# Cross-attention in a decoder layer: the null key and value subtracted in the fold, two score banks, and one softmax pass over 16 heads

## The chip, the cores and the metric

One NeuronCore of a Trainium2 chip runs the whole layer. The metric is the device time of one execution in microseconds (us). TensorE is called PE below, VectorE DVE, ScalarE ACT, GpSimd POOL and the engine that issues the transfers SP.

## The reference, cut to what matters

The input x is 4 x 1024 rows of 256. Three blocks follow each other, each behind a layer norm and with a residual: a gated linear scan, a cross-attention with 16 heads of 64 over 64 context rows per batch, and a feed-forward block of 1024 hidden columns with quantised activations and ternary weights. The change is in the cross-attention:

```
q = heads(x @ Wq) * DH**-0.5;  k, v = heads(context @ Wkv)      # 64 keys and values per head
k = concatenate((null_kv[0], k));  v = concatenate((null_kv[1], v))   # one null key and value for all heads
attn = softmax(q @ k.T)                                         # over 65 keys
out = (attn @ v) @ Wout;  out = layernorm(out)
x = x + out;   x = x + ffn(layernorm(x))
```

## The kernel before, in words

The rows are 32 tiles of 128. Stage 1 (the scan, eight groups of four tiles) runs first. Then the **fold**: Wq is multiplied with the keys of each head, and the values with Wout, so that the scores of a tile are one product of the normed tile (256 wide) with a folded matrix M, and the attention's output one product of the probabilities with VW. M is kept as a high and a low part (Mhi, Mlo), and so is the tile (xT2hi, xT2lo): three products stand for one in float32. Per head M has J = 65 columns, 64 keys and the null key, which is the same for each batch. Its columns come from null_key (L996 on, on DVE). The null value goes through a selection matrix nvsel (L1017 on, 16 small DVE copies) and the product null_values (L1397) into VWnull.

Then stages 2 and 3 run as one software pipeline, stages2_3(n), n from -2 to 31, each engine in its own written order. Nothing is planned at run time: the order in each engine's function and the semaphores set everything. Step n does on PE, in this order: the scores of tile n+2 (two halves, each of two banks with 4 heads x 65 = 260 columns, 24 products in all, banks 0 to 3); the transposes of the probabilities of tile n (banks 4 and 5, L1510 and L1518) and of their null part (L1524); the gate and the up product of the feed-forward block for tile n-5 (gate_up, banks 0, 1 and then 2, 3); the attention's output of tile n (16 products with VW, L1534 and L1539, and one with VWnull, L1540); in even steps the transposes of two more tiles (L1412); and the down product of tile n-7. All scores, gate, up and down products have one line, L1270. Steps 0 to 4 ("filling") have no feed-forward work; there the second half of the scores stands behind the transposes.

DVE's step n is: for each half of tile n+2 the maximum over each head's 65 columns (L1068) and the subtraction of it (L1071), the low part of the null probabilities (L1174), in odd steps xT2lo (L1046), the sum of the exponentials of tile n+1 (L1080), statistics, the hidden layer of the feed-forward block (L1093) which reads the up product, its maximum (L1100), the statistics of the attention's output (L1198), small scales, and the residual (L1152). ACT takes the exponential (L843) of a tile once both halves are subtracted. POOL divides by the sum (L554, and L557 for the null part).

Which wait holds which bank matters here. PE's gate product waits until the first half's scores are subtracted, the up product until the second half's are:

```
pe.wait_ge(sim_sub, upto(2 * n + 5, 2 * T))      # before gate, banks 0 and 1
pe.wait_ge(sim_sub, upto(2 * n + 6, 2 * T))      # before up, banks 2 and 3
```

Of the kernel before, what the change touches and what calls it, by code (L numbers as in the profile page):

```python
# [19 lines left out]
F32 = mybir.dt.float32  # L20
F32R = mybir.dt.float32r
# [12 lines left out]
def decoder_layer(nc, x, ctx_in, w_qkva, gamma, Wq, Wkv, null_kv, Wout, ln_scale, ln_bias,  # L34
# [15 lines left out]
    BANKS_S = 4  # L50
    HB = H // BANKS_S
# [3 lines left out]
    assert (KD, GT, DH, MK, H, N // GN) == (2, 4, 64, 64, 16, 2) and BM == 256 and HB * J <= 512  # L55
# [4 lines left out]
    with ExitStack() as stack:  # L60
# [19 lines left out]
        NP = 5 * H  # L80
        VWnull = sbuf("VWnull", [NP, D], F32R)
        pTn = sbuf("pTn", [NP, P], F32R)
# [25 lines left out]
        nk_bc = sbuf("nk_bc", [P, DH])  # L108
        mnull = sbuf("mnull", [P, KD, H])
        nv = sbuf("nv", [P, 1])  # L110
# [20 lines left out]
        with ExitStack() as early:  # L131
            region_w = early.enter_context(nc.sbuf_tensor("region_w", [P, KD * B * H * J], F32))
# [10 lines left out]
        Mhi = sbuf("Mhi", [P, KD, B, H * J], F32R)  # L143
        Mlo = sbuf("Mlo", [P, KD, B, H * J], F32R)
        region_c = sbuf("region_c", [P, 3968])
# [4 lines left out]
        def carve(region, spec):  # L150
            views, at = {}, 0
            for name, n in spec:
# [12 lines left out]
                             ("nvsel", HC * NP), ("nq", FI // 2), ("nhT", FI // 2)])  # L165
        nvsel = c["nvsel"]
# [15 lines left out]
        def slot_of(h):  # L182
# [20 lines left out]
                             ("xn", 4 * D), ("e", 2 * H * J), ("p", 2 * (H * MK + NP)), ("pT", HC * P),  # L203
# [59 lines left out]
        nkwq_done = sem("nkwq_done")  # L263
        mnull_done = sem("mnull_done")
        mnull_put = sem("mnull_put")
        nvsel_zero = sem("nvsel_zero")
        fT_psum = sem("fT_psum")
# [6 lines left out]
        mnull_hi = sem("mnull_hi")  # L274
        xT2_lo_ready = sem("xT2_lo_ready")
        nv_set = sem("nv_set")
        vwn_psum = sem("vwn_psum")
        vwn_ready = sem("vwn_ready")
# [12 lines left out]
        max_done = sem("max_done")  # L291
        sim_sub = sem("sim_sub")
# [4 lines left out]
        pTn_psum = sem("pTn_psum")  # L297
        pT0_psum = sem("pT0_psum")
        pT1_psum = sem("pT1_psum")
        pTn_hi = sem("pTn_hi")  # L300
        pTn_ready = sem("pTn_ready")
        vwn_hi = sem("vwn_hi")
# [89 lines left out]
        def _(sp):  # L392
# [7 lines left out]
            def weight_T(i, wT):  # L400
# [22 lines left out]
            sp.dma_start(nk_bc[:, :], null_kv[0:1, :].broadcast_to([P, DH])) \  # L423
                .then_inc(null_loaded, 16)
            sp.dma_start(nv[0:DH, :], null_kv[1].rearrange("(d o) -> d o", o=1)) \
                .then_inc(null_loaded, 16)
# [65 lines left out]
        def _(pool):  # L492
# [19 lines left out]
            def stage1(g, u):  # L512
# [13 lines left out]
                if isinstance(g, int) and g == NG - 2:  # L526
                    rounded(0)
                    rounded(1)
# [339 lines left out]
        def _(dve):  # L868
# [724 lines left out]
```

## Time and profile before

| | us |
|---|---|
| time, median of 3 runs (lowest, highest) | 513.25 (513.17, 515.15) |
| span of the profiled execution | 510.8 |
| PE busy | 476.4 (93%) |
| DVE busy | 416.6 (82%) |
| ACT busy | 334.4 (65%) |
| POOL busy | 314.1 (61%) |

The profiled execution's own time is not given beside its span; the median of the timed runs is 2.45 us above the span, which is what lies around it. PE's busy time counts the modelled ends of pipelined products, so distances between the starts of instructions are the better measure, and the rows give both. The granted clock of PE over the span is 0.990 of full speed.

### The profile page before, as it was taken

The numbers are of one execution on the slowest core, as the hardware profiler recorded it, in microseconds if no ns is written. First come the engines' busy times: TensorE is split into PE (matmuls) and PEld (weight loads), VectorE is DVE, ScalarE is ACT, GpSimd is POOL, SyncE is SP. The second block draws the span as 40 slices with busy tenths as digits, with TensorE's granted clock in tenths as the row PEclk, the third lists the DMA queues.
The fourth block names the chain that finished last, engine by engine and source line by source line (L and its number), as shares of the span: only waits on it lengthen the run. The fifth ranks groups of instructions, "written<-read, shape, count | busy, mean of one in ns | idle before, by whom it ended". The sixth has DMA issues, their size and how long they took to land.

```text
span 510.8 us, 8856 instructions
## 1 busy us (share of the span) xinstructions
PE 476.4 (93%) x2934; PEld 390.5 (76%) x2962; DVE 416.6 (82%) x933; ACT 334.4 (65%) x461; POOL 314.1 (61%) x486
## 2 busy tenths in 40 slices
PE   1999999999997998999999999999999999999774
PEld 0778888877676887888888888888888888887432
DVE  4789898968437558799999899898998998997786
ACT  3556652245333334788888888888897888787562
POOL 2234546510003457788787887887878778788861
PEclk9999999999999999999999999999999999999979
DMA  8996000320000000011122211313132212221234
GB/s 256 324 360 255 3 0 1 72 52 2 0 1 1 1 1 7 6 27 42 36 52 45 50 39 38 58 42 49 36 50 46 53 37 52 44 52 37 63 85 117
DMA packets 67116, 31.80 MB, mean 62 GB/s; under 512 B 49664, under 2 KB 65280, under 8 KB 67072
## 3 DMA queue, kind: packets, MB, share of 16 engines
q1 hardware_dynamic: 67072, 31.24, 24.5%
q8 instruction: 24, 0.39, 0.3%
q14 instruction: 20, 0.16, 0.1%
HBM read 15.24 MB, written 4.19 MB: 38 GB/s over the span
## 4 chain that ended last, share of the span: by engine, by line
PE 74%; DVE 11%; POOL 4%; DMA 3%; issue 3%; SPq 2%; ACT 2%; DVEq 0%; POOLq 0%; ACTq 0%
PE psum L1270 33%; PE psum L1534 10%; PE psum L1539 9%; PE psum L1286 9%; DMA xs<-in_x_dram 3%; PE psum L1510 2%; PE psum L1518 2%; SPq L397 2%; PE psum L1412 2%; PE psum L1391 1%; PE psum L1305 1%; DVE den L1080 1%; PE psum L1374 1%; DVE region_d L1071 1%; DVE mx L1068 1%
## 5 line engine op out<-in xcount | busy, mean ns | idle before, releaser
L554 POOL TENSOR_TENSOR region_d<-region_d,rden 128x1024 f32<-128x1024 f32 x32 | 60.9, 1903 | 74.9 <-DVE rden L1085 74.9
L1270 PE MATMUL psum<-Mhi,xT2hi 128*128 128x260 f32 x256 | 75.9, 297 | 0.2
L1270 PE MATMUL psum<-Mlo,xT2hi 128*128 128x260 f32 x256 | 72.9, 285 | 0.0
L1270 PE MATMUL psum<-Mhi,xT2lo 128*128 128x260 f32 x256 | 72.9, 285 | 0.0
L1534 PE MATMUL psum<-VW,region_d 128*128 128x256 f32 x256 | 61.2, 382 | 3.2 <-DVE pTn L1174 3.2
L1539 PE MATMUL psum<-VW,region_d 128*128 128x256 f32 x256 | 60.5, 379 | 0.0
L1534 PEld LDWEIGHTS psum<-VW,region_d 128*128 128x128 f32 x256 | 48.3, 191 | 13.1 <-DVE pTn L1174 4.5
L1068 DVE TENSOR_REDUCE mx<-psum 128x8 f32<-128x520 f32 x64 | 44.5, 696 | 13.0 <-PE psum L1270 11.4
L1539 PEld LDWEIGHTS psum<-VW,region_d 128*128 128x128 f32 x256 | 48.6, 190 | 6.6
L1093 DVE SCALAR_TENSOR_TENSOR region_c<-psum,zw,region_c 128x1024 f32<-128x1024 f32 x32 | 41.0, 1283 | 12.5 <-ACT region_c L768 10.9
L1270 PEld LDWEIGHTS psum<-Mhi,xT2hi 128*128 128x128 f32 x256 | 48.7, 190 | 1.3 <-issue 0.9
L1270 PEld LDWEIGHTS psum<-Mlo,xT2hi 128*128 128x128 f32 x256 | 48.9, 191 | 0.0
L1270 PEld LDWEIGHTS psum<-Mhi,xT2lo 128*128 128x128 f32 x256 | 48.8, 190 | 0.0
L1071 DVE TENSOR_TENSOR region_d<-psum,mx 128x520 f32<-128x520 f32 x64 | 44.8, 699 | 2.2
L843 ACT ACTIVATE region_d<-region_d 128x1040 f32<-128x1040 f32 x32 | 34.3, 1072 | 10.8 <-DVE region_d L1071 10.5
L516 POOL TENSOR_TENSOR pw_out<-pw_in,expo 128x8 f32<-128x8 f32 x8 | 13.2, 1647 | 43.7 <-DVE pw_in L912 43.7
L1100 DVE TENSOR_REDUCE amax<-region_c 128x1 f32<-128x1024 f32 x32 | 39.0, 1219 | 0.9
L1080 DVE TENSOR_REDUCE den<-region_d 128x16 f32<-128x1040 f32 x32 | 39.4, 1230 | 0.4
L768 ACT ACTIVATE region_c<-psum,zw 128x1024 f32<-128x1024 f32 x32 | 35.6, 1114 | 2.7 <-PE psum L1270 2.2
L780 ACT ACTIVATE region_c<-region_c,qr 128x1024 int16<-128x1024 f32 x31 | 35.3, 1139 | 2.8 <-DVE qr L1145 2.4
L571 POOL CAST region_d<-region_c 128x1024 bf16<-128x1024 int16 x31 | 32.2, 1038 | 4.8 <-ACT region_c L780 4.8
L822 ACT ACTIVATE region_d<-psum 128x512 f32<-128x512 f32 x32 | 19.1, 596 | 23.2 <-PE psum L1510 23.2
(151 smaller groups left out, 1217.5 us busy)
## 6 DMA issues: line engine op xcount, KB each, us to landing
out_dram<-xs SPq DMA_DIRECT2D x32, 128.0 KB, 1.9
xs<-in_x_dram SPq DMA_DIRECT2D x1, 2560.0 KB, 13.4
VW<-in_L_xattn_Wkv_dram SPq DMA_DIRECT2D x1, 2048.0 KB, 12.2
region_b<-in_L_xattn_Wkv_dram SPq DMA_DIRECT2D x1, 2048.0 KB, 18.4
xs<-in_x_dram SPq DMA_DIRECT2D x3, 512.0 KB, 7.4
region_w<-in_L_ffn_w_gate_dram SPq DMA_DIRECT2D x2, 512.0 KB, 10.3
region_w<-in_L_ffn_w_up_dram SPq DMA_DIRECT2D x2, 512.0 KB, 7.7
region_w<-in_L_ffn_w_down_dram SPq DMA_DIRECT2D x8, 128.0 KB, 5.1
```

The source lines that it names most:

```text
L554: pool.tensor_tensor(p2[:, v, 0:H * MK].rearrange("p (h j) -> p h j", j=MK), e[:, :, 0:MK], rden[:, v, :].unsqueeze(2).broadcast_to([P, H, ...
L768: act.activation(hid3[v], banks(0, 2).rearrange("p b n -> p (b n)"), ACT.Silu, scale=zw[:, (n - 5) % 4, 0:1]).then_inc(silu_ready, 1)
L780: act.activation(nq3, hid3[t % 2], ACT.Copy, scale=qr[:, t % 2, 0:1]).then_inc(hq_done, 1)
L1068: dve.tensor_reduce(mx[:, hh, :].rearrange("p (b h) -> p b h", h=HB), scores, AX.X, ALU.max) \
L1071: dve.tensor_tensor(e2[:, u, hh * 2 * HB * J:(hh + 1) * 2 * HB * J].rearrange("p (b h j) -> p b h j", b=2, j=J), scores, mx[:, hh, :].rear ...
L1080: dve.tensor_reduce(den[:, :], e2[:, slot, :].rearrange("p (h j) -> p h j", j=J), AX.X, ALU.add) \
L1093: dve.scalar_tensor_tensor(out=hid3[v], in0=banks(2, 2).rearrange("p b n -> p (b n)"), scalar=zw[:, (n - 5) % 4, 1:2], in1=hid3[v], op0=AL ...
L1100: dve.tensor_reduce(amax[:, v, 0:1], hid3[v], AX.X, ALU.max, apply_absolute_value=True) \
L1270: mm = pe.matmul(dst, lhsT, rhs, start=i == 0, stop=i == len(terms) - 1)
L1286: mm = pe.matmul(bank(b), lhsT, rhs, start=i == 0, stop=i == len(terms) - 1)
L1534: pe.matmul(bank(7, D), pT[:, pair, :], VW[:, batch(n), pair, :], start=pair == 0, stop=False)
L1539: pe.matmul(bank(7, D), pT[:, pair, :], VW[:, batch(n), pair, :], start=False, stop=False)
```

## The change

The softmax does not change when the same number is subtracted from all scores of a head. The change subtracts the null key from every key and the null value from every value when they are copied out of the projection (ACT's put_kvT, now with a bias). The null score is then zero, needs no columns, and M has 64 columns per head. The null value becomes one row that is added to each output: the sum of Wout over the heads, times the null value (wsum on POOL, then one product into vnull), which goes in with one product with a matrix of ones ahead of the 16 with VW.

The scores of 8 heads are 512 columns, one bank: six products per half, 12 per tile, in banks 0 and 1. The gate product moves to banks 2 and 3, the up product to 0 and 1. The exponential's input needs the shift in column 64 of each head: -max(0, maximum), a new small operation on DVE, and the shift is added to the scores. From step 5 on (tile 7 on) DVE does both halves at once: one maximum, one shift, one addition over 16 heads. The transposition, copy and low part of the null probabilities, their division on POOL, null_key, and nvsel's 16 copies are gone. The waits for the VW copies move from the second half of tile 0's scores to the transposes of tile 0's probabilities.

```diff
-            sp.dma_start(nk_bc[:, :], null_kv[0:1, :].broadcast_to([P, DH])) \
-            sp.dma_start(nv[0:DH, :], null_kv[1].rearrange("(d o) -> d o", o=1)) \
-            sp.dma_start(nv[DH:P, :], null_kv[1].rearrange("(d o) -> d o", o=1)) \
+            for i in range(2):
+                sp.dma_start(nulls[0:DH, i:i + 1], null_kv[i].rearrange("(d o) -> d o", o=1)) \
+                sp.dma_start(nulls[DH:P, i:i + 1], null_kv[i].rearrange("(d o) -> d o", o=1)) \
...
# POOL, in and behind stage 1
+                    pool.tensor_scalar(nulls_neg[:, :], nulls[:, :], -1.0, 0.0, ALU.mult, ALU.add) \
-            pool.memset(nvsel, 0.0).then_inc(nvsel_zero, 1)
+            pool.tensor_tensor(wsum, wout[:, 0, :], wout[:, 1, :], ALU.add).then_inc(wout_summed, 1)
+            for pair in range(2, HC):
+                pool.wait_ge(wout_summed, pair - 1)
+                pool.tensor_tensor(wsum, wsum, wout[:, pair, :], ALU.add).then_inc(wout_summed, 1)
# POOL, probabilities
-                pool.tensor_tensor(p2[:, v, H * MK:].rearrange("p (m h) -> p m h", h=H),
-                                   e[:, :, MK].unsqueeze(1).broadcast_to([P, NP // H, H]),
-                                   rden[:, v, :].unsqueeze(1).broadcast_to([P, NP // H, H]), ALU.mult) \
# ACT
-                act.activation(kvT[:, i % 4, :], bank(i % 2, BM), ACT.Copy).then_inc(kvT_ready, 1)
+                act.activation(kvT[:, i % 4, :], bank(i % 2, BM), ACT.Identity, bias=nulls_neg[:, null:null + 1]) \
-                act.activation(hid3[v], banks(0, 2).rearrange("p b n -> p (b n)"), ACT.Silu,
+                act.activation(hid3[v], banks(2, 2).rearrange("p b n -> p (b n)"), ACT.Silu,
-                    act.wait_ge(pTn_psum, n + 1)
-                    act.activation(pTn[:, :], psum[0:NP, 7, D:D + P], ACT.Copy).then_inc(pTn_hi, 1)
# DVE
-                if i in (2, 4):
-                    null_key((i - 2) // 2)
-                if i == 6:
-                    null_values()
+            def softmax_both(n, u):
+                scores = banks(0, 2).rearrange("p b (h j) -> p (b h) j", j=MK)
+                e = e2[:, u, :].rearrange("p (h j) -> p h j", j=J)
+                dve.wait_ge(sim_psum, 2 * n + 2)
+                dve.wait_ge(p_ready, n - 1)
+                dve.tensor_reduce(mx[:, :, :].rearrange("p a h -> p (a h)"), scores, AX.X, ALU.max).then_inc(max_done, 2)
+                dve.wait_ge(max_done, 2 * n + 2)
+                dve.tensor_scalar(e[:, :, MK], mx[:, :, :].rearrange("p a h -> p (a h)"), 0.0, -1.0, ALU.max, ALU.mult) \
+                    .then_inc(shift_done, 2)
+                dve.wait_ge(shift_done, 2 * n + 2)
+                dve.tensor_tensor(e[:, :, 0:MK], scores, e[:, :, MK].unsqueeze(2).broadcast_to([P, H, MK]), ALU.add) \
+                    .then_inc(sim_sub, 2)
...
-                if exists(n + 2, T):
+                if exists(n + 2, T) and n >= 5:
+                    softmax_both(n + 2, u)
+                if exists(n + 2, T) and n < 5:
                     softmax_half(n + 2, 0, u)
...
-                    dve.wait_ge(pTn_hi, n + 1)
-                    lo = pTn[2 * H:3 * H, :]
-                    dve.tensor_tensor(lo, psum[2 * H:3 * H, 7, D:D + P], lo.bitcast(F32), ALU.subtract) \
-                        .then_inc(pTn_ready, 1)
# PE, scores_half
-                for g in (2 * hh, 2 * hh + 1):
-                    mm = group(bank(g, HB * J),
+                group(bank(hh), [(xT[:, (u4 // 2) % 2, k, (u4 % 2) * P:(u4 % 2 + 1) * P],
+                                  m[:, k, b, hh * HB * MK:(hh + 1) * HB * MK])
# PE, gate_up
-                pe.wait_ge(sim_sub, upto(2 * n + 5, 2 * T))
-                    mm = group(bank(j), [(nT3[:, slot, k, :], wgT[:, k, j * 512:(j + 1) * 512]) for k in range(KD)])
+                    mm = group(bank(2 + j), [(nT3[:, slot, k, :], wgT[:, k, j * 512:(j + 1) * 512]) for k in range(KD)])
-                pe.wait_ge(sim_sub, upto(2 * n + 6, 2 * T))
                 for j in range(2):
-                    mm = group(bank(2 + j), [(nT3[:, slot, k, :], wuT[:, k, j * 512:(j + 1) * 512]) for k in range(KD)])
+                    pe.wait_ge(sim_sub, upto(2 * n + 5 + j, 2 * T))
+                    mm = group(bank(j), [(nT3[:, slot, k, :], wuT[:, k, j * 512:(j + 1) * 512]) for k in range(KD)])
# PE, stages2_3
-                    pe.transpose(psum[0:NP, 7, D:D + P], p2[:, u, H * MK:], ident[:, :]).then_inc(pTn_psum, 1)
-                    pe.wait_ge(pTn_ready, n + 1)
+                    if positive(n):
+                        pe.wait_ge(y2_ready, n)
+                    if n == 0:
+                        pe.wait_ge(vnull_ready, 1)
+                    pe.matmul(bank(7, D), ones_r[:, :], vnull[:, :], start=True, stop=False)
...
-                    pe.matmul(bank(7, D), pTn[:, :], VWnull[:, :], start=False, stop=True).then_inc(out_psum, 1)
```

## Rows read from the trace of the kernel before

**Rows 1.** The page: busy us, share of the span and instructions of each engine.
```profile
PE 476.4 (93%) x2934; PEld 390.5 (76%) x2962; DVE 416.6 (82%) x933; ACT 334.4 (65%) x461; POOL 314.1 (61%) x486
```
**Rows 2.** Two stretches: length, busy PE, PEld, DVE, ACT, POOL, granted clock, DMA.
```profile
163.00:168.00 5.00, 3.72 (x17) 3.64 (x18) 2.08 (x5) 1.25 (x3) 2.26 (x2) 0.66 0.00 0
225.00:453.00 228.00, 226.85 (x1476) 193.90 (x1497) 207.24 (x430) 195.60 (x253) 184.69 (x309) 1.00 0.22 45
```
**Rows 3.** The chain that ended last, two steps apart: start us, us, what.
```profile
421.43 3.78 PE psum L1270 x32
...
442.17 3.78 PE psum L1270 x32
```
**Rows 4.** Timeline of PE in step 28: start us, us, instruction.
```profile
442.81 0.37 PE L1270 MATMUL psum<-Mhi,xT2hi 128*128 128x260 f32 x1
...
445.66 0.28 PE L1270 MATMUL psum<-Mhi,xT2lo 128*128 128x260 f32 x1
...
447.63 1.03 PE L1270 MATMUL psum<-wuT,region_d 128*128 128x512 bf16 x4
...
452.87 0.37 PE L1270 MATMUL psum<-Mhi,xT2hi 128*128 128x260 f32 x1
```
**Rows 5.** Timeline of DVE in the same step.
```profile
444.57 0.69 DVE L1068 TENSOR_REDUCE mx<-psum 128x8 f32<-128x520 f32 x1
...
446.72 0.70 DVE L1071 TENSOR_TENSOR region_d<-psum,mx 128x520 f32<-128x520 f32 x1
447.45 0.28 DVE L1174 TENSOR_TENSOR pTn<-psum,pTn 16x128 fp32r<-16x128 f32 x1
...
450.28 1.28 DVE L1093 SCALAR_TENSOR_TENSOR region_c<-psum,zw,region_c 128x1024 f32<-128x1024 f32 x1 [0.73 <-ACT region_c L768]
```
**Rows 6.** Groups of instructions by form: busy us, mean ns, idle before.
```profile
L1286 PE MATMUL psum<-xT1hi,w1lo 128*128 128x512 f32 x96 | 30.1, 396 | 0.0
L972 DVE TENSOR_TENSOR region_a<-psum,region_a 128x1024 f32<-128x1024 f32 x8 | 9.8, 1223 | 0.7 <-PE psum L1286 0.3
L1100 DVE TENSOR_REDUCE amax<-region_c 128x1 f32<-128x1024 f32 x32 | 39.0, 1219 | 0.9
L911 DVE TENSOR_SCALAR pw_in<-mv 128x4 f32<-128x4 f32 x8 | 1.4, 170 | 0.3
```
**Rows 7.** The chain: runs of products back to back.
```profile
48.98 4.12 PE psum L1286 x18
...
206.47 2.87 PE psum L1270 x24
...
446.82 0.11 PE psum L1524
```
**Rows 8.** The fold's last keys: timeline of DVE, ACT and PE.
```profile
127.06 3.08 DVE L1023 COPY region_c<-nv 64x3 f32<-64x3 f32 x16
...
128.56 1.10 ACT L719 ACTIVATE Mhi<-psum 128x512 fp32r<-128x512 f32 x2 [1.98 <-PE psum L1374]
...
131.61 1.96 PE L1391 MATMUL psum<-region_b 64*64 64x256 f32 x32 [1.17 <-DVE Mlo L1030]
```
**Rows 9.** Step 0: timeline of POOL, DVE and PE.
```profile
160.42 0.39 POOL L557 TENSOR_TENSOR region_d<-region_d,rden 128x80 f32<-128x80 f32 x1
...
163.81 0.42 DVE L1169 TENSOR_TENSOR VWnull<-psum,VWnull 16x256 fp32r<-16x256 f32 x1
...
164.28 0.43 PE L1524 MATMUL psum<-ident,region_d 128*80 128x128 f32 x1 [2.32 <-DVE VWnull L1169]
...
167.12 2.02 PE L1534 MATMUL psum<-VW,region_d 128*128 128x256 f32 x8
```
**Rows 10.** Step 3: timeline of PE.
```profile
192.67 0.28 PE L1270 MATMUL psum<-Mhi,xT2lo 128*128 128x260 f32 x1
...
193.65 1.99 PE L1534 MATMUL psum<-VW,region_d 128*128 128x256 f32 x8 [0.69 <-DVE pTn L1174]
```
**Rows 11.** The chain: the output products of the fifth tile.
```profile
202.20 1.99 PE psum L1534 x8
```

More of the change, by code:

```diff
@@ L77, in decoder_layer @@
         VW = sbuf("VW", [P, B, HC, D])
-        NP = 5 * H
-        VWnull = sbuf("VWnull", [NP, D], F32R)
-        pTn = sbuf("pTn", [NP, P], F32R)
+        NR = DH // 2 + 1
+        vnull = sbuf("vnull", [NR, D], F32R)
+        ones_r = sbuf("ones_r", [NR, P], F32R)
         wgT = sbuf("wgT", [P, KD, FI], BF16)
@@ L501, in _ @@
             pool.memset(ones[:, :], 1.0).then_inc(consts_set, 1)
+            pool.memset(ones_r[:, :].bitcast(F32), 1.0).then_inc(consts_set, 1)
+            pool.memset(nvsel[:, :], 0.0).then_inc(nvsel_zero, 1)
             pool.wait_ge(consts_set, 2)
@@ L814, in stages2_3 @@
                 if n == 0:
-                    act.wait_ge(vwn_psum, 1)
-                    act.activation(VWnull[:, :], psum[0:NP, 7, 0:D], ACT.Copy).then_inc(vwn_hi, 1)
+                    act.wait_ge(vnull_psum, 1)
+                    act.activation(vnull[:, :], psum[0:NR, 7, 0:D], ACT.Copy).then_inc(vnull_hi, 1)
                 if exists(n, T):
@@ L1092, in hidden_layer @@
                 dve.wait_ge(silu_ready, n - 4)
-                dve.scalar_tensor_tensor(out=hid3[v], in0=banks(2, 2).rearrange("p b n -> p (b n)"),
+                dve.scalar_tensor_tensor(out=hid3[v], in0=banks(0, 2).rearrange("p b n -> p (b n)"),
                                          scalar=zw[:, (n - 5) % 4, 1:2], in1=hid3[v], op0=ALU.mult, op1=ALU.mult) \
@@ L1163, in stages2_3 @@
                     exp_sum_reciprocal(n + 1, v)
-                if exists(n + 2, T) and not filling(n):
+                if n < 0:
                     softmax_half(n + 2, 1, u)
                 if n == 0:
-                    dve.wait_ge(vwn_hi, 1)
-                    lo = VWnull[4 * H:NP, :]
-                    dve.tensor_tensor(lo, psum[4 * H:NP, 7, 0:D], lo.bitcast(F32), ALU.subtract).then_inc(vwn_ready, 1)
-                if exists(n, T):
-                    dve.wait_ge(pTn_hi, n + 1)
-                    lo = pTn[2 * H:3 * H, :]
-                    dve.tensor_tensor(lo, psum[2 * H:3 * H, 7, D:D + P], lo.bitcast(F32), ALU.subtract) \
-                        .then_inc(pTn_ready, 1)
+                    dve.wait_ge(vnull_hi, 1)
+                    lo = vnull[NR - 1:NR, :]
+                    dve.tensor_tensor(lo, psum[NR - 1:NR, 7, 0:D], lo.bitcast(F32), ALU.subtract).then_inc(vnull_ready, 1)
                 if filling(n):
@@ L1395, in fold_values, with null_values @@
                 mm.then_inc(fold_psum, 1)
-            def null_values(first, end):
-                pe.wait_ge(nv_set, 2 * HC)
-                for pair in range(first, end):
-                    mm = pe.matmul(psum[0:NP, 7, 0:D], nvsel[:, pair * NP:(pair + 1) * NP], wout[:, pair, :],
-                                   start=pair == 0, stop=pair == HC - 1)
-                return mm
+            def null_values():
+                pe.wait_ge(nv_set, 2)
+                pe.wait_ge(wout_summed, HC - 1)
+                pe.matmul(psum[0:NR, 7, 0:D], nvsel[:, :], wsum, start=True, stop=True).then_inc(vnull_psum, 1)
             def pair_T(q, r):
```

142 lines of the change are left out of this document (54 added, 88 removed).

## The prediction
> **What bounds the kernel now.** I read the busy shares first: PE is busy 93% of the span, DVE 82% [rows 1]. A share over the whole span doesn't say which of the two sets the time, so I took the table by stretch: from 225 to 453 us PE is busy 226.85 of 228, DVE 207.24, and the granted clock is 1.00 (2.4 GHz) [rows 2]. There PE starts instruction after instruction, and the chain of waits runs over PE alone: from one step to the second after it, it takes 442.17 - 421.43 = 20.74 us, so 10.37 a step [rows 3]. DVE is close behind, and whatever makes PE wait there lengthens every step.
>
> The timeline of step 28 is the pattern [rows 4]. Its scores start at 442.81, the last of the 24 products at 445.66; transposes and the gate product follow, the up product starts at 447.63, and the next step at 452.87, 10.06 after this one (steps that also transpose two more tiles are longer). From the scores' start (0), up starts at 4.82, and from there 5.24 are left. On DVE the first maximum starts at 444.57, while PE still computes the second half, and the second subtraction ends at 446.72 + 0.70 = 447.42 [rows 5]. Up starts 0.21 later and had only just to wait, if at all: DVE's softmax lies wholly beside PE's scores, transposes and gate.
>
> **The change, part by part.** *PE's own work.* 24 products of 260 columns take 2.87 back to back, 0.120 each; 18 of 512 columns take 4.12, 0.229 each [rows 7]. So 12 x 0.229 = 2.75: 0.12 less a tile. The null transposition is 0.11 [rows 7] and goes. The null product stays, first in its group now and with 33 rows in place of 80; columns are the same 256, so I count nothing. Without a wait a step of PE would be 0.23 shorter.
>
> *DVE's softmax from step 5 on.* The wait for the scores is now one for both halves. The last product starts at (2.97 - 0.12) - 0.23 = 2.62, where 2.97 is the scores' length in step 28 (445.66 + 0.12 - 442.81) [rows 4]. It ends 0.40 later [rows 6], and DVE starts 0.03 after that: 3.05. Then a maximum over 1024 columns, 1.22 like the other reduction of that size [rows 6]; the shift over 16 columns, 0.18, nearest to the 0.170 of a 4-column operation [rows 6], with 0.28 as the upper bound from the 128-column one [rows 5]; the addition, 1.22 like the one that reads two banks [rows 6]; and two gaps of 0.03 between operations that wait for each other. That is 2.68, so the pass ends at 5.73.
>
> *The wait that this makes.* The up product moves to banks 0 and 1, the banks of the scores, and needs the whole pass. PE is in order: up, the 16 output products, the down product and the next scores all stand behind it. PE has its transposes and the gate to do meanwhile, so up could start at 4.82 - 0.23 = 4.59. It gets its banks at 5.73 and, by the 0.21 of step 28, starts at 5.94. PE waits 1.35. The rest of the step is unchanged: 5.94 + 5.24 = 11.18 against 10.06, 1.12 more. The same holds for all steps 5 to 29, 25 of them, the longer ones too. In the first two DVE holds PE up already, which makes no more than a few tenths of difference. 25 x 1.12 = 28.0; I take 27.5. Nothing later in DVE's step takes over: hidden layer began at 450.28 after a wait of 0.73 for ACT [rows 5], 2.86 after the second subtraction ended; 5.73 + 2.86 - 0.31 (the null part's low part, gone) = 8.28, earlier by far than the next scores at 11.18, which now need it for both halves. Bounds: if the gap to up is 0.05 and not 0.21, 24 for the 25 steps; with the shift at 0.28, 30.
>
> At this place the Trainium skill speaks for the change: "VectorE: DVE Perf Modes", section "Rules for kernel authors", says of chained DVE operations to minimise their number. The change does that, five per tile to three. By that rule alone each tile would gain about 0.4 us of DVE; that is rival C below, and the rows above have PE, not DVE, without idle time.
>
> *The fold.* 16 small copies of the null value occupy DVE for 3.08 from 127.06 [rows 8], and the last low parts of M stand behind them; PE waits 1.17 for these at 131.61. The ACT copies that they need end at 128.56 + 1.10 = 129.66. Without the small copies the last low part would run 129.66 to about 130.3, and PE starts some 1.0 earlier; that is also all PE's wait. null_key on DVE goes too, beside PE's products, which don't wait for it: 0. Of PE's 16 null products the first eight stand where DVE and ACT copy VW, which they mostly hide: 0.1. Together 1.1 less, bounds 0.5 and 1.5. The bias on ACT's copies costs nothing that I count, same engine and size. wsum's seven additions of 256 columns on POOL replace a memset and lie where POOL is idle until 158 us. Of small loads on SP there are four for three, ahead of Wv's values, which PE needs much later; 0.
>
> *Steps -2 to 0.* Tiles 0 and 1 go through a latency chain (scores, DVE, ACT, DVE, POOL, PE), where two shifts cost 0.2 each, and a third one behind POOL. POOL's null division, 0.39 [rows 9], is gone from it. Then DVE makes VWnull's low part, 163.81 + 0.42 = 164.23, PE transposes the null part at 164.28, has 12 products of scores left, and starts the outputs at 167.12 [rows 9]. In the new order those scores don't stand behind the null part: they run while DVE works, and the outputs can start right behind the new low part (same 256 columns), at 164.23 + 0.2 + 0.05 = 164.5. That is 2.6 less. PE's own gap just gets another place, and after the old one its clock fell: 0.66 in 163 to 168 [rows 2]. If it falls again ahead of the scores, about 1 is lost. I take 2.2 less, bounds 1 and 3.
>
> *Steps 1 to 4.* The output products wait for the null part: in step 3 the last score starts at 192.67 and ends its turn at 192.79, the outputs start at 193.65 [rows 10], 0.86 lost. In steps 0 to 4 they start at 167.12 [rows 9], ..., 202.20 [rows 11]: 8.77 a step. With the wait gone (0.86), the transposition (0.11) and the shorter scores (0.12, given back in part by transitions) the step is some 7.9. DVE has two shifts more in each and comes close to that. 4 x 0.85 = 3.4 less, bounds 1.5 and 4.
>
> *The end.* Without scores there is no stall. The chain runs over POOL, ACT and DVE; POOL loses its null division (0.39 [rows 9]) once or twice, DVE 0.28 [rows 5] twice. 0.7 less, bounds 0 and 1.5.
>
> **The sum** on the profiled execution: 510.8 - 1.1 - 2.2 - 3.4 + 27.5 - 0.7 = 530.9. The median of the runs shown is 2.45 above that execution's span; so 533.3.
>
> **The rivals.** *B: the clock falls.* The new gap of 1.35 comes every step. After the gap of 2.32 in step 0 [rows 9] the five us around it had 0.66, that is some 1.7 us lost. If each of the 25 gaps did that, the time would be 533.3 + 25 x 1.7 = 576. Against it: the gaps are shorter by 1 us, and PE works 88% of a step; 0.69-us gaps in each of steps 1 to 4 [rows 10] left full speed around them. Chance 0.05.
>
> *C: faster.* DVE sets the steady step after all, and PE's missing idle time only shows that both are equally loaded. Then the fewer DVE operations shorten it. This is what the Trainium skill's rule would give. The mechanism needs the pass to end by 4.59, 1.14 earlier than worked out, so that up isn't held; then a step is 0.23 shorter, 25 x 0.23 = 5.8, and with 7.4 from the other parts the time is 513.25 - 13.2 = 500.1. For it: DVE is at 91% in the steady stretch [rows 2], and the hidden layer has slack of only 0.73. Against it: a maximum and an addition over 1024 columns can't overlap the scores, and 1.22 each is measured. Chance 0.05.
>
> *D: half of the stall is hidden,* for instance because reads of 1024 columns in two banks with whole heads are quicker than the 1.22 rows. If the pass ends at 5.0, the stall is 0.62 and a step 0.39 longer: 9.8 in all, against 7.4 less elsewhere: 515.6. It turns from slower to faster at 0.30 a step. Chance 0.04.
>
> **How the numbers follow.** The forecast, 0.86: its own range is 27.5 with -4 and +3, the other parts -7.4 with +4 and -2.5, so 526 to 540. B, C and D lie outside, together 0.14. This kernel's measurement tells about 0.5% (2.6 us) from no change. Slower is the forecast and B (0.91) and half of D, 0.93; same is 0.02; faster is C, 0.05.
>
> **What would show it.** In the new profile PE's up product, in every step from 5 to 29, has idle time of 1.2 to 1.5 us that ends with DVE's addition; the distance between steps is 11.2 and 11.8 in turn. DVE has 1 to 2 us of idle time before each maximum over 1024 columns, which itself is 1.2. The 512-column scores start every 0.23. The outputs of steps 1 to 4 no longer wait for DVE, and their distance is near 7.9. PE's fold starts its value products near 130.6. The prediction is wrong if up starts within 0.3 us of the gate's end, or if the granted clock of the steady stretch is below 1.00.

## The result and the profile after

| | before | after |
|---|---|---|
| time, median of the runs (lowest, highest) | 513.59 (513.17, 515.15) | 554.99 (554.50, 556.58) |
| span of the profiled execution | 510.8 | 553.0 |
| PE, DVE busy | [rows 1] | 483.3 (87%), 403.4 (73%) |

The change makes the kernel slower by a factor of 1.0794, 95% interval 1.0763 to 1.0826. The forecast was 533.3, range 526 to 540: the direction is right, the size is not. 42.2 of span came on top, where 20.1 were worked out. All medians and ratios here and below are of fast runs; one run of tt_shift (560.10) was in the slow state.

The page of after, busy time by engine (PE had 93% in [rows 1], DVE 82%):
```profile
PE 483.3 (87%) x2532; PEld 363.8 (66%) x2532; DVE 403.4 (73%) x864; ACT 328.9 (59%) x429; POOL 308.5 (56%) x465
```
PE and DVE both have a smaller share than before, and in each step each of them now waits for the other, as the rows below show. PE's waits, by what ended them (us in total, times, longest):
```profile
PE psum L1246 <- DVE region_d L1054: 36.1, 25, 1.7
```
L1246 is the up product, L1054 the addition over 16 heads: 25 steps, 1.44 each in the mean. The forecast had this wait, 25 times 1.35. PE's timeline over one step:
```profile
328.01 1.03 PE L1246 MATMUL psum<-wgT,region_d 128*128 128x512 bf16 x4
330.54 1.02 PE L1246 MATMUL psum<-wuT,region_d 128*128 128x512 bf16 x4 [1.50 <-DVE region_d L1054]
331.49 0.38 PE L1498 MATMUL psum<-vnull,ones_r 33*128 33x256 f32 x1
331.80 1.99 PE L1501 MATMUL psum<-VW,region_d 128*128 128x256 f32 x8
...
335.36 1.04 PE L1246 MATMUL psum<-wdT,region_d 128*128 128x256 bf16 x8
336.15 0.48 PE L1246 MATMUL psum<-Mhi,xT2hi 128*128 128x512 f32 x1
...
338.76 0.39 PE L1246 MATMUL psum<-Mhi,xT2lo 128*128 128x512 f32 x1
...
342.24 1.02 PE L1246 MATMUL psum<-wuT,region_d 128*128 128x512 bf16 x4 [1.35 <-DVE region_d L1054]
```
DVE in the same step:
```profile
339.25 1.22 DVE L1049 TENSOR_REDUCE mx<-psum 128x16 f32<-128x1024 f32 x1 [1.70 <-issue]
340.58 0.18 DVE L1051 TENSOR_SCALAR region_d<-mx 128x16 f32<-128x16 f32 x1
340.86 1.22 DVE L1054 TENSOR_TENSOR region_d<-psum,region_d 128x1024 f32<-128x1024 f32 x1
```
From the scores' start, 336.15, the pass ends at 340.86 + 1.22 = 342.08, 5.93 later (forecast 5.73), and up starts at 6.09 (5.94). DVE sat idle 1.70 until the last score of both halves was done, then PE sat idle 1.35 until DVE was done. Before, the first maximum ran while PE computed the second half [rows 5], and the first subtraction and the second maximum followed it beside PE's last scores and transposes:
```profile
445.29 0.70 DVE L1071 TENSOR_TENSOR region_d<-psum,mx 128x520 f32<-128x520 f32 x1
445.98 0.70 DVE L1068 TENSOR_REDUCE mx<-psum 128x8 f32<-128x520 f32 x1
```
But from up's start to the down product are 335.36 - 330.54 = 4.82; before it was 452.07 - 447.63 = 4.44, where 452.07 is the down product of step 28:
```profile
452.07 1.05 PE L1270 MATMUL psum<-wdT,region_c 128*128 128x256 bf16 x8
```
From up to up a step takes 342.24 - 330.54 = 11.70 here and 12.30 the next time, 24.00 for two; the forecast was 11.2 and 11.8 in turn, 23.0.

Where the 42.2 lie, by the start of the output products on the chain: up to the first, 2.3 less (165.00 here); from there to the fifth tile's [rows 11], 1.3 less; from the fifth to the thirtieth, 44.7 more; behind that, 1.1 more. So the loss is in the steps that I forecast, and 17.2 larger than forecast. By the profile's idle times the 44.7 are waits for DVE 36.1, 25 x 0.38 = 9.5 from up to down, the clock some 3.4 (below), less some 5.7 that were worked out for PE's shorter work; that leaves 1.4 open. By the forecast's own terms it closes: 28.0 by the sum that was cut to 27.5, 25 x 0.15 = 3.8 because up starts at 6.09 and not at 5.94, 9.5 and 3.4. The 0.38 had no explanation, and the experiments began with it.

### The profile page after: what moved, and what is told of

Its sections match the earlier page's. It is cut to its first block, busy times and chain, and to the rows that moved or that the text cites. A ratio compares the mean times of both kernels' runs of the same rounds, so it can differ in the third digit from the quotient of the medians.

```text
span 553.0 us, 7919 instructions
## 1 busy us (share of the span) xinstructions
PE 483.3 (87%) x2532; PEld 363.8 (66%) x2532; DVE 403.4 (73%) x864; ACT 328.9 (59%) x429; POOL 308.5 (56%) x465
## 4 chain that ended last, share of the span: by engine, by line
PE 61%; DVE 20%; issue 11%; ACT 2%; DMA 2%; POOL 2%; SPq 1%; DVEq 0%; ACTq 0%; POOLq 0%
PE psum L1246 21%; PE psum L1262 11%; PE psum L1501 11%; PE psum L1506 9%; DVE region_d L1054 6%; DVE mx L1049 6%; PE psum L1498 2%; PE psum L1350 2%; PE psum L1367 1%; PE psum L1281 1%; PE psum L1297 1%; PE psum L1386 1%; DVE region_d L1051 1%; DVE xs L1132 1%; DMA gcol<-in_L_attn_gamma_dram 1%
## 5 line engine op out<-in xcount | busy, mean ns | idle before, releaser
L1501 PE MATMUL psum<-VW,region_d 128*128 128x256 f32 x256 | 67.3, 408 | 0.1
L1049 DVE TENSOR_REDUCE mx<-psum 128x16 f32<-128x1024 f32 x25 | 30.6, 1225 | 46.6 <-issue 44.5
L1246 PE MATMUL psum<-wuT,region_d 128*128 128x512 bf16 x128 | 32.8, 378 | 36.1 <-DVE region_d L1054 36.1
L1506 PE MATMUL psum<-VW,region_d 128*128 128x256 f32 x256 | 62.1, 387 | 0.0
L1246 PE MATMUL psum<-Mhi,xT2hi 128*128 128x512 f32 x128 | 53.7, 420 | 1.1 <-DVE region_d L1040 0.8
L1246 PE MATMUL psum<-Mhi,xT2lo 128*128 128x512 f32 x128 | 50.4, 394 | 0.0
L1246 PE MATMUL psum<-Mlo,xT2hi 128*128 128x512 f32 x128 | 50.0, 390 | 0.0
L1246 PEld LDWEIGHTS psum<-wuT,region_d 128*128 128x128 bf16 x128 | 10.6, 96 | 57.1 <-issue 45.6
L760 ACT ACTIVATE region_d<-psum,sc 128x256 f32<-128x256 f32 x32 | 17.9, 559 | 39.6 <-POOL sc L596 39.5
L1246 PE MATMUL psum<-wgT,region_d 128*128 128x512 bf16 x128 | 32.9, 379 | 5.9 <-DMA region_d<-region_c 5.9
L752 ACT ACTIVATE xT2hi<-psum 128x512 fp32r<-128x512 f32 x16 | 9.6, 599 | 43.1 <-PE psum L1386 43.1
```

What stands on the lines that cost most here:

```text
L1049: dve.tensor_reduce(mx[:, :, :].rearrange("p a h -> p (a h)"), scores, AX.X, ALU.max).then_inc(max_done, 2)
L1246: mm = pe.matmul(dst, lhsT, rhs, start=i == 0, stop=i == len(terms) - 1)
L1501: pe.matmul(bank(7, D), pT[:, pair, :], VW[:, batch(n), pair, :], start=False, stop=False)
L1506: mm = pe.matmul(bank(7, D), pT[:, pair, :], VW[:, batch(n), pair, :], start=False, stop=pair == HC - 1)
```

## The experiments

All kernels are changed from after, but for one that is changed from before. "Ratio" is to the kernel before on the same chip (514.1 to 514.3 there); the runs were made on three chips, so kernels are compared by their ratios.

| kernel | us, median | ratio, 95% interval |
|---|---|---|
| null_last | 555.58 | 1.0791, 1.0739 to 1.0844 |
| halves | 517.21 | 1.0065, 1.0038 to 1.0092 |
| up_late | 512.65 | 0.9969, 0.9944 to 0.9995 |
| merged_before | 561.96 | 1.0924, 1.0870 to 1.0977 |
| tt_shift | 555.45 | 1.0802, 1.0758 to 1.0847 |
| tt_null_last | 552.74 | 1.0769, 1.0742 to 1.0795 |
| tt_null128 | 540.19 | 1.0510, 1.0486 to 1.0535 |
| best | 499.24 | 0.9707, 0.9683 to 0.9732 |
| late_null128 | 503.89 | 0.9798, 0.9774 to 0.9823 |
| halves128 | 501.47 | 0.9753, 0.9731 to 0.9775 |
| best_h | 496.85 | 0.9671, 0.9644 to 0.9697 |

**halves: the pass over 16 heads is taken back, all else stays.**
```
-                if exists(n + 2, T) and n >= 5:
-                    softmax_both(n + 2, u)
-                if exists(n + 2, T) and n < 5:
+                if exists(n + 2, T):
                     softmax_half(n + 2, 0, u)
 ...
-                if n < 0:
+                if exists(n + 2, T) and not filling(n):
                     softmax_half(n + 2, 1, u)
```


> The changed kernel with the softmax by halves in all steps, so one maximum, shift and addition over 8 heads twice. Theory 1 (the stall of 1.44 us a step at the up product comes from waiting for one pass over both halves): the first half is done long before up needs bank 0, the second about when it needs bank 1, stall 0.1 to 0.4, step 10.8 instead of 12.0, time 525. Theory 2 (DVE's number of operations sets the step, halves add three per tile, about 0.6 us): slower than 555, some 565 or more. Theory 3 (two score banks alone make the wait, whatever the pass): 550 to 555.

Measured 517.21, 8 less than theory 1 had. With 554.99 that puts the merging at 1.0794 - 1.0065 = 7.3%, 37.5 us. PE's wait for the addition of a half in this kernel, its largest for DVE in the steady stretch (200 to 490 us):
```profile
PE psum L1244 <- DVE region_d L1040: 3.2, 9, 0.4
```
So the merging makes the long wait. These 3.2 don't hold all of DVE's part, though, because up's second half needs the second bank. A shift that POOL holds (below) puts it off, here by DVE, then PE:
```profile
353.76 0.63 DVE L1038 TENSOR_SCALAR region_d<-mx 128x8 f32<-128x8 f32 x1
```
```profile
354.22 0.59 PE L1244 MATMUL psum<-wuT,region_d 128*128 128x512 bf16 x2
355.17 0.61 PE L1244 MATMUL psum<-wuT,region_d 128*128 128x512 bf16 x2 [0.36 <-DVE region_d L1040]
```
From up to the null product it is 1.49 there, and 0.96 in steps where the shift takes 0.18. Still, by the forecast's other terms (7.4, and 5.8 for the shorter work of PE) this kernel should have been some 13 us faster than before, and it is 0.65% slower: a second sign of something else that costs.

**merged_before: the kernel before, only maximum and subtraction merged, over its four banks.**
```
-                if exists(n + 2, T):
+                if exists(n + 2, T) and n >= 5:
+                    softmax_both(n + 2, u)      # maximum and subtraction over 4 banks, sim_sub by 2
+                if exists(n + 2, T) and n < 5:
                     softmax_half(n + 2, 0, u)
 ...
-                if exists(n + 2, T) and not filling(n):
+                if n < 0:
                     softmax_half(n + 2, 1, u)
```


> The kernel before with one change: from step 5 on DVE takes the maximum and the subtraction over all four score banks at once (65 columns a head, four banks, null columns as before). Theory 1 (merging the halves is what costs, since PE's next use of the score banks, here the gate product, waits for the whole pass): gate could start 3.95 us after the scores' start and gets its banks at about 5.8, 1.8 us a step in 25 steps, time 555 to 560. Theory 2 (the two score banks and the swapped gate and up banks cost, merging is harmless or saves DVE time): 510 to 515.

Measured 561.96, the slowest of all, and within 2 us of theory 1. Without a shift, without new null products and without another order of PE, the merging costs 9.2%. Here the gate is the first that needs the scores' banks, and it stands earlier than up, so more of the pass lies bare. PE's waits and its gate:
```profile
PE psum L1286 <- issue: 48.8, 24, 2.4
```
```profile
331.23 0.27 PE L1540 MATMUL psum<-ident,region_d 128*80 128x128 f32 x1
333.52 0.81 PE L1286 MATMUL psum<-wgT,region_d 128*128 128x512 bf16 x3 [2.02 <-issue]
```
The wait is named "issue" and not DVE: the releaser isn't always inferred, and the idle time in brackets, right at the end of DVE's subtraction (331.96 + 1.24 = 333.20), is what to read.

**up_late: the same pass, but up stands between the two groups of eight output products.**
```
                 if exists(n + 2, T) and exists(n - 5, T):
-                    gate_up(n, v)
+                    gate(n, v)
 ...          # null product, 8 output products
+                if exists(n + 2, T) and exists(n - 5, T):
+                    up(n, v)
 ...          # 8 output products
```


> The changed kernel, the softmax over 16 heads kept, but PE computes the up product of steps 5 to 29 between the first and the second eight output products. Theory 1 (PE only waits because nothing else stands between the scores and up): the stall goes, step about 10.6, time 519, 36 us less. Theory 2 (the later up product delays the hidden layer on DVE and so the next scores, the wait only moves): next scores wait for the hidden layer or DVE idles more; 535 to 555.

Measured 512.65, ratio 0.9969, 6 less than theory 1 had. 1.99 of PE's own work now covers what remained of DVE's pass, and PE shows no wait for it: up, at 333.00, follows the output products that began at 330.95 for 1.99. So the 36 us were no work that DVE lacks time for, but a place in PE's order. Again the kernel isn't the 13 us faster that its parts would give.

**null_last: the null product behind the 16 output products, where it stood before.**
```
-                    pe.matmul(bank(7, D), ones_r[:, :], vnull[:, :], start=True, stop=False)
 ...          # 16 output products, the first with start=True
+                    pe.matmul(bank(7, D), ones_r[:, :], vnull[:, :], start=False, stop=True)
```


> The changed kernel with the null product put back behind the 16 output products. Theory 1 (its place costs PE a fixed time when a float32r product is followed by float32 ones; from up's start to down's start a step takes 4.82 us now and 4.44 before): 0.38 us less in each of some 30 steps, 11 us in all, so about 544 against 555. Theory 2 (the longer step is all DVE's pass, the place is worth nothing): 555, and up to down still 4.8 in the trace.

Measured 555.58, no difference from after (both intervals lie over each other). From up to the next product behind the group it was 4.72 for 4.82. Its place isn't the cause. The equal times hide something, though: the outputs of the thirtieth tile start 3.3 earlier than in after (496.3 for 499.6), because the clock doesn't fall before (last section), and from there to the end it is 3.4 longer, at a granted clock of 0.85 where after has 0.96.

**tt_shift, tt_null_last, tt_null128: the shift in another form, and the null factors with 128 rows.** The shift is zeros minus maximum, two tensors in, the clip at zero left out; the third has this too:
```
-        vnull = sbuf("vnull", [NR, D], F32R)       # NR = 33
-        ones_r = sbuf("ones_r", [NR, P], F32R)
+        vnull = sbuf("vnull", [P, D], F32R)        # zeros besides rows 0 and 32
+        ones_r = sbuf("ones_r", [P, P], F32R)
```


> The changed kernel with the shift written as a DVE tensor_tensor (zeros minus the maximum) in place of a tensor_scalar; the clip at zero is left out, which changes the shift but not the softmax. Theory P (the shift waits while POOL works on SBUF: its duration went from 0.18 to 1.5 us in the changed kernel, 0.265 in the mean over the 25 late steps and 0.541 over the 14 early halves; a form that doesn't wait for POOL stays at its 0.18): all shifts 0.17 to 0.20, the late steps shorten by 0.08 on average, the early ones by some 2 to 3 us together, total 4 to 5 us less, 550 against 555. Theory N (the durations have nothing to do with the form): the same spread, up to 0.5 us and more, and 555.

> As the run with the tensor_tensor shift, and the null product behind the output products. With the tensor_scalar form the place of the null product changed nothing in the total (555.6), but the median of the shift had gone from 0.18 to 0.64 us. Theory P (0.1 us a step won on PE was lost again to shifts that wait for POOL): now the shifts are 0.18 and the gain of 0.1 us in 32 steps shows, 3 us under the run with the tensor_tensor shift alone. Theory N: no difference to it, 550 to 555.

> As the run with the tensor_tensor shift, and the null product's two factors have 128 rows (zeros but in rows 0 and 32, so the same value) in place of 33; it stays in front. Theory R (a product of 33 rows can't have its weights loaded beside the product ahead of it, nor the next one's beside it: weight loads start 0.31 to 0.42 us late around it in the trace; with 128 rows like its neighbours they overlap): up's start to down's start falls from 4.82 to 4.45 us, 0.3 to 0.38 in each of 32 steps, 10 to 12 us under the run with the tensor_tensor shift alone, about 539. Theory T (the change of number format between bfloat16, float32r and float32 costs): 4.8 us and no difference.

tt_shift is 555.45 and tt_null_last 552.74: neither differs from after by more than 0.5%, and the form of the shift isn't the matter. The two differ by 2.7, near the 3 of theory P; but their intervals overlap, and tt_null_last's shifts are held more and not less (456 ns in the mean of the 25 late ones, tt_shift 277), so theory P's reason is not borne out. tt_null128 is 540.19, 2.9% less than tt_shift (1.0510 against 1.0802), for a product with four times the rows. At least 3.0 of the 17.6 us between the two spans are not the rows': they lie ahead of the first null product (166.49 and 163.49), and tt_shift had a fall of the clock there (0.91 from 30 to 50 us). The summary of the null product's line in after (duration min/median/max, then idle time before it by what ended it) shows what went:
```profile
L1498 PEld LDWEIGHTS psum<-vnull,ones_r x32: 182/183/183, 164.6 to 515.2; 33*128 33x128 f32 x32
L1498 PE MATMUL psum<-vnull,ones_r x32: 379/381/385, 164.6 to 515.2; 33*128 33x256 f32 x32
its engine sat idle before it (us, times) until:
  issue: 12.2, 30
```
The loads of weights in after (PEld):
```profile
331.49 0.18 PEld L1498 LDWEIGHTS psum<-vnull,ones_r 33*128 33x128 f32 x1 [0.42 <-issue]
331.80 1.59 PEld L1501 LDWEIGHTS psum<-VW,region_d 128*128 128x128 f32 x8
```
and in tt_null128:
```profile
331.00 0.19 PEld L1503 LDWEIGHTS psum<-vnull,ones_r 128*128 128x128 f32 x1
331.21 0.95 PEld L1506 LDWEIGHTS psum<-VW,region_d 128*128 128x128 f32 x5
```
In after the load for the null product starts after 0.42 without a load, as late as its product (331.49), and 0.31 behind the start of up's last product (331.18); the first load for VW stands with its own product too (331.80). In tt_null128 the load for the null product starts with up's last product (331.00), and the next load 0.21 later, 0.12 ahead of its product (331.33). From up to the null product it is 0.95 in after and 0.67 in tt_null128, and the 16 products behind take 0.11 less: together the 0.39 by which the time from up to the next product behind the group falls, 4.43 for 4.82. So a product of 33 rows between products of 128 rows takes its load of weights, and its neighbour's, out of the overlap. The null product of before had 80 rows and showed no such gap: its load started with the last output product, at 451.73, and its own start is 0.03 behind that.

The Trainium skill, "TensorEngine Tiling (Array Packing)", section "Key Properties", says that a change of the tiling mode drains TensorE. The gap would fit that if 33 rows run in another mode than 128; which mode they run in, no run shows.

The trace of before already had the like. In the fold, products of 64 rows follow products of 128 and are followed by them; PEld sat idle ahead of both changes:
```profile
105.91 0.73 PEld L1374 LDWEIGHTS psum<-region_b,VW 64*128 64x128 f32 x8 [0.33 <-issue]
106.98 1.59 PEld L1270 LDWEIGHTS psum<-region_b,VW 128*128 128x128 f32 x8 [0.33 <-issue]
```
The products' starts lie 0.31 apart at each change and 0.32 at the next, and 0.22 among products of 128 rows: the same 0.31, 0.31, 0.32 that stand around the null product of 33 rows.

**halves128: halves, with 128 null rows. late_null128: up_late, with 128 null rows.**

> The changed kernel with the softmax over two halves in every step (no merging) and null factors of 128 rows; up stays where it is. Theory R: the halves alone were 517.2; PE waited for DVE only 3.9 us in all, so most of 30 x 0.4 = 12 comes off: 505 to 508, 6 to 8 faster than the kernel before. Rival (DVE, with five operations a tile and shifts that wait for POOL, sets the step, so PE's shorter work turns into waiting): 513 to 517.

> The changed kernel with the up product between the two groups of eight output products, and null factors of 128 rows; the shift and its clip stay as they are. It splits the 55.8 us by which the kernel with all three edits (128 rows, late up, no separate shift) beat the changed one. Theory R (PE is without a stall, so a step is PE's own work and 0.4 of the null product's surroundings goes from each of 30): late up alone was 512.7, less 30 x 0.4 = 12, so 500 to 502, and the shift is worth 2 at most because nothing waits for DVE. Rival S (with the null product cheap, DVE's pass is what is late next, and the shift that waits for POOL decides): 505 to 509, and PE shows a wait for DVE's addition.

Measured 501.47 and 503.89. halves128 lies 3.5 below all that was expected of it: the 128 rows bring 1.0065 - 0.9753 = 3.1%, 16 us, half a microsecond in each of 32 steps. That is more than the 0.39 a time, 12.5 us, that the starts around the product show. The rest goes with the shifts: from step 5 on POOL holds them for less (204 ns in the mean, halves 359), so up's second half waits less, and from up to the null product it is 0.72 in the mean for 1.23, of which 0.28 are the rows'. The summary of its null product names no idle time but that of the first two:
```profile
L1496 PE MATMUL psum<-vnull,ones_r x32: 279/469/469, 164.6 to 460.9; 128*128 128x256 f32 x32
its engine sat idle before it (us, times) until:
  DVE vnull L1149: 3.7, 2
```
late_null128 lies above the 500 to 502 of theory R and below rival S: the rows bring 1.7% there (9 us), not the 2.3% forecast, and no wait for DVE's addition shows, so S is no explanation either. Its steady steps are as long as those of halves128 (9.97 and 9.99 in the mean). The 2.9 between the two spans lie behind the start of the thirtieth tile's outputs, where the granted clock (third number from the end) was lower; late_null128, then halves128:
```profile
444.70:502.40 57.70, 42.47 (x212) 26.43 (x214) 40.60 (x95) 29.79 (x34) 34.00 (x58) 0.86 0.33 70
```
```profile
445.40:499.50 54.10, 39.01 (x209) 24.72 (x210) 38.74 (x93) 28.95 (x34) 32.58 (x56) 0.91 0.37 74
```
What makes the clock fall more there is not shown.

**best and best_h: 128 rows, late up, and the maximum written negated into its place, so that no shift is needed; best_h with two halves in every step.** The clip of the maximum at zero goes with the shift; best also counts the negated maximum by one, on a semaphore of its own.
```
-                dve.tensor_reduce(mx[:, hh, :], scores, AX.X, ALU.max).then_inc(max_done, 1)
-                dve.wait_ge(max_done, 2 * n + hh + 1)
-                dve.tensor_scalar(e[:, :, MK], mx[:, hh, :], 0.0, -1.0, ALU.max, ALU.mult).then_inc(shift_done, 1)
+                dve.tensor_reduce(e[:, :, MK], scores, AX.X, ALU.max, negate=True).then_inc(shift_done, 1)
```


> The changed kernel with three edits: up between the halves of the outputs, the null product with 128 rows, and no shift operation (the maximum is written negated into column 64, so the clip at zero is left out). By the theory of the stall and theory R: step 10.42 as measured with up moved, less 0.35 is 10.1; 512.7 less 0.35 x 32 = 11 is 501.5, less 1 to 3 for the early shifts, so 499 to 502. If DVE becomes the bound (it has 9.6 to 9.9 us of work a step and waits for the scores), steps stay at 10.3 and the time at 506 or more.

> The kernel with all three edits (128 null rows, late up, maximum written negated so that no shift is needed), but with the softmax over two halves in every step: is the merging worth anything once nothing waits for it? Theory M0 (PE sets the step; DVE's saved fixed costs only become idle time): 499 to 501, the same as with merging (499.2) within 0.5%. Rival M+ (DVE is close enough behind that its fewer operations count): 503 to 508. Rival M- (earlier ends of the first half free a bank and help): 494 to 497.

Measured 499.24 and 496.85; both beat the kernel before, by 2.9% and 3.3%. The merging is worth nothing once nothing waits for it (0.9707 against 0.9671, intervals that just overlap). best_h landed in the 494 to 497 of M-, not in M0's 499 to 501, but M-'s reason is not what the traces show: the steady steps are 9.92 and 9.94 in the mean, the same, and of the 2.6 between the two spans 1.8 lie behind the start of the thirtieth tile's outputs, at a granted clock of 0.96 in best_h and 0.90 in best. So M0's reason holds for the steps, and its number doesn't. The page of best_h:
```profile
PE 460.9 (93%) x2504; PEld 360.8 (73%) x2532; DVE 393.9 (80%) x875; ACT 328.9 (66%) x429; POOL 307.6 (62%) x465
```
PE has its 93% again, in a span of 495.1. Its gate products, two steps apart, start at
```profile
400.12 1.03 PE L1239 MATMUL psum<-wgT,region_d 128*128 128x512 bf16 x4
...
420.28 1.03 PE L1239 MATMUL psum<-wgT,region_d 128*128 128x512 bf16 x4
```
20.16 for two steps, where [rows 3] has 20.74: 0.29 less a step, and the forecast for a step without the stall was 0.23 less.

**The shift and POOL.** After has 39 shifts, and each takes 0.18 unless an operation of POOL is already running when it starts. The first that was held, DVE, then POOL:
```profile
158.93 1.50 DVE L1038 TENSOR_SCALAR region_d<-mx 128x8 f32<-128x8 f32 x1
160.46 0.69 DVE L1040 TENSOR_TENSOR region_d<-psum,region_d 128x512 f32<-128x512 f32 x1
```
```profile
158.49 1.90 POOL L560 TENSOR_TENSOR region_d<-region_d,rden 128x1024 f32<-128x1024 f32 x1 [44.96 <-DVE rden L1065]
```
POOL's division ends at 160.39, the shift at 160.43; at 175.83, 184.03, 206.86 and 352.73 it is the same, each end 0.02 to 0.04 after POOL's. One that starts at 244.59, 0.01 ahead of POOL's operation, takes 0.18, and so does one at 189.19 beside a POOL operation on a single column. The maximum over scores in PSUM isn't held (158.26, 0.63). The Trainium skill, "SBUF — State Buffer", section "SBUF: two separate sides", says that DVE and GpSimd share a pair of ports as an exclusive lock, and that the one who comes second is blocked for the whole instruction, DVE only with a two-port mode or two SBUF inputs. The ends agree. After's shift has one SBUF input, so by the page it would have to run in a two-port mode, and no view here shows an operation's mode. tt_shift's has two, and it is held neither more nor less (means of 277 and 496 ns for the two passes, after 265 and 541).

## Why the prediction was right and where it was wrong

*The wait at up: right.* Place, cause, count and nearly the size: 25 x 1.44 against 25 x 1.35. The 0.20 by which the pass ended later (5.93 for 5.73) lie in the three gaps of the pass: 0.10 or 0.11 before the maximum, the shift and the addition, where I took 0.03. The cause of these gaps is open. One reading was wrong without a consequence here: the null transposition was taken at 0.11, but the gate started 0.33 behind it, so the gate now starts 0.46 earlier (339.86 - 336.15 = 3.71 behind the scores' start, before 4.17) and not 0.23. While DVE sets up's start, this is idle time only. By experiment the merging is worth 37.5 where the forecast's terms give 27.5 + 5.8 = 33.3.

*The null product: the step that failed.* "The null product stays, first in its group now and with 33 rows in place of 80; columns are the same 256, so I count nothing." It costs 0.38 a step, from up to down: 9.5 in the 25 steady steps and 12 in all. Three pairs of kernels, alike within the pair but for the rows, put it at 16 us (halves, halves128), 15 (tt_shift, tt_null128) and 9 (up_late, late_null128); the larger two hold other things too, the shifts held for longer and a fall of the clock ahead of any null product. The span lies 22.1 over the 530.9 that were worked out: 17.2 in the steady steps (9.5 the null product, 3.8 the later end of DVE's pass, some 3.4 the clock, 0.5 the cut from 28.0 to 27.5), 2.1 in steps 1 to 4 (five null products, 1.9), 1.0 before them and 1.8 at the end, which I did not take apart. So the null product makes over half of the miss. The clock's falls, which neither halves nor tt_null128 has in its steady steps, bring it to some seven tenths; their cause is open. I had priced a product by its columns alone, a price of 0 without bounds. The trace of before could have bounded it: the products of 64 rows in the fold show 0.31, 0.31 and 0.32 for 0.22 at a change of rows, three times 0.1 for each such group. The place, which I named too, costs nothing in the step (null_last).

*PE without the stall: right in the sum, in part by luck.* Rival C's time, 500.1, was the sum of all the gains with no wait. halves128, which comes nearest to that case, has 501.47. But the parts offset each other: up to the first output products 2.3 less (3.3 worked out), steps 1 to 4 4.2 less (3.4), the 25 steady steps 6.5 less (5.8), and the end 1.8 longer where 0.7 less was worked out.

*Single parts.* The fold's value products start at 131.23, not 130.6, where [rows 8] has 131.61:
```profile
130.62 0.94 ACT L715 ACTIVATE region_b<-psum,nulls_neg 128x256 f32<-128x256 f32 x2
...
131.23 0.61 PE L1367 MATMUL psum<-region_b 64*64 64x256 f32 x5 [0.19 <-ACT region_b L715]
```
The 16 small copies are gone as forecast, but ACT's high part of M ends at 130.25 and not 129.66, the last low part at 131.09 and not 130.3, and PE then waits for ACT's copy above, which I had not followed. The first output products start at 165.00, 2.3 earlier than before where 3.3 were forecast for fold and first steps, and one shift there took 1.50 beside POOL's division, where I had priced each at 0.2. In steps 1 to 4 only 1.3 of 3.4 came: five null products of 33 rows. Two more shifts were held there, for 1.48 and 1.44, but halves128 has such shifts too and gains 4.2.

*Rival B, the clock: much smaller than its price, but there.* I had named a granted clock below 1.00 in the steady stretch as a sign that the prediction is wrong. From 252 to 490 us it was 1.00, but between 200 and 252, in the first steady steps, it fell, as it did in step 0; the sign appeared, at a price of about 3 us (length, busy PE, PEld, DVE, ACT, POOL, granted clock, DMA):
```profile
163.00:171.00 8.00, 6.39 (x23) 5.25 (x24) 4.28 (x8) 1.17 (x4) 1.90 (x1) 0.79 0.01 2
200.00:252.00 52.00, 46.09 (x216) 34.55 (x215) 37.45 (x73) 32.52 (x41) 34.09 (x54) 0.93 0.09 20
252.00:490.00 238.00, 209.18 (x1087) 156.88 (x1086) 178.92 (x348) 172.94 (x209) 159.36 (x259) 1.00 0.19 40
```
There eight output products took 3.40 and 3.51 in place of 1.99 in steps 5 and 7: 3 us in all, a little more with their neighbours.

*D is excluded.* Reads of 1024 columns over two banks take 1.22, as the rows of before said.

*The range* was 526 to 540, and the time lies 15 above it. It rested on the bounds of the terms that I had, and a term that I set to zero had none. With the rows at 128 the same change measures 540.19 (with the other form of shift), at the range's upper edge: the other misses use up what the bounds allowed.

## What to carry to other kernels

Before operations of one engine are merged, look at which engine waits for their results and whether the first of them ran beside that engine's work: two passes with half the banks each let PE and DVE overlap, and one pass of the same cost made PE wait 36 us. Where a merging does make a wait, look for work of the waiting engine that needs nothing of it and put it first; that took the whole wait back here. Price a matmul by its rows as well as its columns, and look in the trace at hand for any change of rows between neighbours. Here the factors padded to the 128 rows of the neighbours took 0.3 to 0.6 us off each steady step. And before two kernels with nearly equal times are called equal, compare them by stage: a fall of the clock in one and not in the other is worth 2 to 3 us here.

## What was not expected of the hardware

- A product of 33 rows between products of 128 rows: 0.4 us of idle time of the weight loads ahead of it each time (12.2 in 30 times) and the following load not overlapped; 0.39 us a time. 64 rows show the same spacing in the fold, 80 rows don't.
- The clock's fall in step 0 doesn't go by the wait alone. PE's wait ahead of the null product is 1.62 in halves128 and 1.63 in after, and halves, with 33 rows, has 0.79 from 163 to 171 us, as after has. null_last waits 1.63 too, but runs eight products with VW behind the wait and its 33 rows only later, and has 1.00. The kernel before, with 80 rows and a wait of 2.32, has 0.79. halves128:
```profile
163.00:171.00 8.00, 6.44 (x36) 5.67 (x37) 4.96 (x10) 3.00 (x6) 2.99 (x4) 1.00 0.01 2
200.00:252.00 52.00, 51.32 (x271) 40.85 (x276) 48.76 (x109) 44.16 (x55) 42.35 (x73) 1.00 0.16 32
```
  Between 200 and 252 us only after falls (0.93): halves, which lacks the long wait, and tt_null128, which keeps it but has 128 rows, both have 1.00 there. Also null_last, with 33 rows and the long wait, has 1.00 there. What decides this is not shown.
- A DVE operation of 8 or 16 columns from SBUF to SBUF was held until POOL's running operation ended, for up to 1.3 us (1.50 for 0.18); the same with one tensor in as with two.
- In the merged pass DVE leaves 0.10 or 0.11 before each operation, also behind the shift of 16 columns, and 0.03 in the pass by halves. merged_before has it too (330.62 + 1.24 to 331.96), and so has best, whose semaphore counts by one. It is not the 1024 columns alone: behind the hidden layer's operation of that size it is 0.03. It stays open what sets it.
